# Weighing and key fills placed behind the maxima of each cycle, and VectorE's long steps of both layers moved behind its maxima

## What is computed

```
x = x + L0_xattn(ln(x), ctx); x = x + L0_attn(ln(x)); x = x + L0_ffn(ln(x))
# L1 cross attention, by far the largest part: 32 x 16 heads x 64 x 1601 scores
k, v = ctx @ Wk.T + bk, ctx @ Wv.T + bv
p = softmax(q / 4 @ k.T);  x = x + (p @ v) @ Wo.T + bo
# L1 "attn": x1 = pw(causal_conv(rmsnorm(ln(x)))) + ..., hg = normed @ w_hg,
#   h_t = a_t * h_(t-1) + v_t  (a scan over the 64 tokens), x2 = h @ w_out + x1, then silu(n @ wg) * (n @ wv) @ w_ff_out
# L1 "ffn": xq = round(x / scale); h = gelu(xq @ W1q); hq = round(h / scale(h)); out = hq @ W2q
```

## Time and profile before

| | |
|---|---|
| time, median of 3 runs (lowest, highest) | 2437.48 us (2430.88, 2440.86) |
| the profiled execution | 2435.09 us, its span 2433.2 us |
| TensorE busy | 2077.9 us, 85% |
| VectorE, ScalarE, GpSimd busy | 1412.0, 1053.6, 519.1 us |
| granted TensorE clock, mean | 0.933 of 2.4 GHz |
| first scores, last scores | 119.96 us, 2350.44 us |

### The profile page before, as it was taken

One profiled execution on the slowest core, in us unless ns is written; L12 is line 12 of the kernel. 1 busy time (PEld: TensorE's weight loads), 2 busy tenths in 40 slices (PEclk: granted clock), 3 DMA queues, 4 the chain that ended last, 5 costly groups with the idle time before them and its releaser, 6 DMA issues.

```text
span 2433.2 us, 72895 instructions
## 1 busy us (share of the span) xinstructions
PE 2077.9 (85%) x31670; PEld 1652.4 (68%) x31686; DVE 1412.0 (58%) x2625; ACT 1053.6 (43%) x2167; POOL 519.1 (21%) x836
## 2 busy tenths in 40 slices
PE   3798988898889899888988988888998889889864
PEld 2676776776767677776777767667776666667643
DVE  3556666656657664665567556565666555554533
ACT  2354445444445444445454444545434343444331
POOL 1222221212222122222212122221222211222100
PEclk7899998899999999999999999989999999999985
DMA  6334332333223243242333232233232202122121
GB/s 194 142 109 159 108 125 92 107 103 123 99 91 112 90 141 116 102 141 71 111 102 116 95 132 98 74 112 116 84 102 88 66 28 86 61 83 64 47 75 44
DMA packets 99115, 243.93 MB, mean 100 GB/s; under 512 B 13168, under 2 KB 19440, under 8 KB 98800
## 3 DMA queue, kind: packets, MB, share of 16 engines
q1 hardware_dynamic: 98800, 239.26, 29.1%
HBM read 235.94 MB, written 3.15 MB: 98 GB/s over the span
## 4 chain that ended last, share of the span: by engine, by line
PE 67%; DVE 23%; issue 5%; ACT 3%; SPq 1%; POOL 1%; DMA 0%; DVEq 0%; POOLq 0%; ACTq 0%
PE M L722 12%; DVE mx L1417 11%; PE SC L917 7%; PE O L940 7%; PE SC L894 7%; PE M L715 7%; PE X L744 4%; PE SC L910 3%; PE M L744 2%; DVE oT L1432 2%; PE X L1000 2%; PE M L785 1%; PE X L971 1%; PE M L749 1%; DVE V L1238 1%
## 5 line engine op out<-in xcount | busy, mean ns | idle before, releaser
L1110 ACT ACTIVATE probT<-SC 128x512 f32<-128x512 f32 (+1 forms) x1024 | 445.6, 522 | 323.5 <-PE SC L917 322.7
L1417 DVE TENSOR_REDUCE mx<-SC 128x4 f32<-128x1600 f32 (+1 forms) x256 | 467.2, 1825 | 167.2 <-PE SC L894 167.1
L1059 ACT ACTIVATE kT<-M,bk 128x400 f32<-128x400 f32 (+1 forms) x224 | 133.4, 595 | 639.8 <-PE M L715 639.7
L722 PE MATMUL M<-wvs,rowsT 128*128 128x256 f32 x2496 | 381.4, 304 | 0.8 <-issue 0.8
L715 PEld LDWEIGHTS M<-rowsT,wks 128*128 128x128 f32 x1536 | 265.6, 190 | 146.5 <-issue 141.5
L715 PE MATMUL M<-rowsT,wks 128*128 128x400 f32 (+1 forms) x1536 | 351.4, 364 | 11.2 <-PE SC L917 10.4
L722 PEld LDWEIGHTS M<-wvs,rowsT 128*128 128x128 f32 x2496 | 333.7, 202 | 31.9 <-issue 12.3
L1238 DVE TENSOR_TENSOR V<-M,bv 128x256 f32<-128x256 f32 (+1 forms) x448 | 160.1, 399 | 271.1 <-PE M L722 266.7
L582 POOL TENSOR_TENSOR rowsT<-raw,rowsT 128x768 fp32r<-128x768 f32 (+1 forms) x128 | 253.5, 1981 | 211.4 <-ACT rowsT L1160 210.4
L894 PE MATMUL SC<-kT,bdq 32*128 32x400 f32 (+1 forms) x2048 | 245.6, 548 | 20.8 <-ACT probT L1110 14.3
L917 PE MATMUL SC<-bdq,kT 32*128 32x128 f32 x6656 | 257.8, 290 | 0.0
(11 more groups left out here) (250 smaller groups left out, 2532.2 us busy)
## 6 DMA issues: line engine op xcount, KB each, us to landing
ring<-in_ws_dram SPq DMA_DIRECT2D x428, 256.0 KB, 4.5
raw<-in_ctx_dram SPq DMA_DIRECT2D x32, 1601.0 KB, 6.7
summed<-in_ctx_dram SPq DMA_DIRECT2D x60, 800.5 KB, 4.5
ring<-rounded_scratch SPq DMA_DIRECT2D x64, 256.0 KB, 6.2
out_dram<-x SPq DMA_DIRECT2D x16, 128.0 KB, 2.2
x<-in_x_dram SPq DMA_DIRECT2D x1, 1792.0 KB, 10.4
kT<-in_ctx_dram SPq DMA_DIRECT2D x2, 800.5 KB, 8.8
rounded_scratch<-wround SPq DMA_DIRECT2D x8, 128.0 KB, 2.0
```

Of the source, the lines that this page charges most:

```text
L722: mm = pe.matmul(bank[:, (t - 2 * a) * D:(t - 2 * a + 1) * D], rowsT[xp][:, cc, t * P:(t + 1) * P], wvs[wp][:, cc, :], start=(at == cc == ...
L1059: act.activation(keys(n, c)[:, k0:k0 + kn], bank[:, 0:kn], ACT.Identity, bias=bk[:, c:c + 1]).then_inc(m_used[f % 2], 1)
L1110: act.activation(probT[step % 2][0:w, j, 0:len(ts), :].rearrange("p t q -> p (t q)"), SC[0:w, j, 0:len(ts) * P], ACT.Exp)\
L1417: dve.tensor_reduce(mx[c][:, :, n], SC[:, :, 0:KCH[n][1]], AX.X, ALU.max).then_inc(max_used, 1)
```

## The change

1. On TensorE, `maxima` moves ahead of `weigh`. Place "B" keeps only `max0` and `max1` and is ahead of the maxima, right behind "A"; sums, output projection and `wabs` go to a place "C" behind `weigh`; the old "C" is now "D".
2. No key chunk is filled ahead of the maxima any more. The first fill of k = 7 is gone; key (1, 2) is second in k = 7, and key (1, 3) second in k = 0 of its own batch, a cycle later. ScalarE drains all keys; 32 drains leave VectorE for ScalarE.
3. On VectorE, the convolution, the recurrence, the rounding of `xq`, `hidden_scale` with the rounding of `hq`, and the start of layer 0's softmax stand behind the maxima and the second drains (`layer1_later`, `softmax_start`). Their readers on TensorE come a cycle later: the steps of layer 1 from `gow` on (q = 9 to 17 become 10 to 18), those of layer 0 from `l0_pt0` on. The `up` and `up0` fills with their Gelu move from k = 7 of an odd batch to k = 0 of the even one.
4. On GpSimd the low part stands ahead of the layers' steps, and the recurrence's operand (`gates`) at the end of the cycle.

```diff
-FIRST = [[value(5)], [value(6)], [value(0)], [value(1)], [value(2)], [value(3)], [value(4)], [key(1, 2)]]
-SECOND = [[], [key(0, 0)], [key(0, 1)], [key(0, 2)], [key(0, 3)], [key(1, 0)], [key(1, 1)], [key(1, 3)]]
+FIRST = [[value(5)], [value(6)], [value(0)], [value(1)], [value(2)], [value(3)], [value(4)], []]
+SECOND = [[key(1, 3)], [key(0, 0)], [key(0, 1)], [key(0, 2)], [key(0, 3)], [key(1, 0)], [key(1, 1)], [key(1, 2)]]
+OWN = value(5), value(6), key(1, 3)
...
-L1_X = {(5, "A"): "conv_in", (6, "A"): "pw", (7, "A"): "gru_in", (7, "C"): "hg0", (8, "A"): "hg1", (9, "A"): "gow",
-        (10, "A"): "ff_in", (10, "C"): "ff0", (11, "A"): "ff1", (11, "C"): "ff2", (12, "A"): "fow", (14, "A"): "xq",
-        (15, "A"): "up0", (17, "A"): "hq", (17, "C"): "down"}
+L1_X = {(5, "A"): "conv_in", (6, "A"): "pw", (7, "A"): "gru_in", (7, "D"): "hg0", (8, "A"): "hg1", (10, "A"): "gow",
+        (11, "A"): "ff_in", (11, "D"): "ff0", (12, "A"): "ff1", (12, "D"): "ff2", (13, "A"): "fow", (15, "A"): "xq",
+        (16, "A"): "up0", (18, "A"): "hq", (18, "D"): "down"}
...
@@ tensor
-                    for what in x_fills(b, k, "A"):
-                        fill_x(what)
+                    for place in "AB":
+                        for what in x_fills(b, k, place):
+                            fill_x(what)
+                    maxima(b, k)
                     if k:
                         weigh(b, k - 1)
                     else:
                         weigh(b - 1, STEPS - 1)
-                    for what in x_fills(b, k, "B"):
+                    for what in x_fills(b, k, "C"):
                         fill_x(what)
-                    maxima(b, k)
                     for what in pieces(b, k, "second"):
                         fill(what)
-                    for what in x_fills(b, k, "C"):
+                    for what in x_fills(b, k, "D"):
                         fill_x(what)
...
@@ vector
-                    for what in x_fills(b, k, "A"):
-                        drain_x(what)
-                    for t, q in second_layer(b, k):
-                        if q == 16:
-                            hidden_scale(t)
+                    for place in "AB":
+                        for what in x_fills(b, k, place):
+                            drain_x(what)
+                    maxima(b, k)
                     if k == 0 and 0 <= b - 1 < B:
                         dve.wait_ge(o_ready, b)
                         dve.tensor_copy(osb[:, :, :], Og).then_inc(o_used, 1)
-                    for what in x_fills(b, k, "B"):
+                    for what in x_fills(b, k, "C"):
                         drain_x(what)
-                    maxima(b, k)
                     for what in pieces(b, k, "second"):
                         drain(what)
+                    for t, q in second_layer(b, k):
+                        layer1_later(t, q)
                     for i, q in first_layer(b, k):
                         if q == 4:
+                            softmax_start(i)
+                        if q == 5:
                             softmax_end(i)
```

More of the change, by code:

```diff
@@ L179, in pieces @@
     for what in (FIRST, SECOND)[half == "second"][k]:
-        batch = b if what in (value(5), value(6)) else b + 1
+        batch = b if what in OWN else b + 1
         if 0 <= batch < B and b >= -1:
@@ L205, in x_fills @@
     if place == "B":
+        if k == 3 and 0 <= b < B:
+            yield "max1", b
+        if k == 7 and 0 <= b + 1 < B:
+            yield "max0", b + 1
+    if place == "C":
         if k == 1 and 0 <= b - 1 < B:
@@ L236, in use, with count @@
             USES.append((what, cycle, name))
+    def count(what, number, kind, cycle):
+        number[what] = len(number)
+        use(what, kind, cycle)
     for b, k in SLOTS:
         cycle = STEPS * b + k
-        for half in ("first", "second"):
-            for what in pieces(b, k, half):
-                NUMBER[what] = len(NUMBER)
-                use(what, what[1], cycle)
-            for place in ("AB" if half == "first" else "C"):
-                for what in x_fills(b, k, place):
-                    XNUMBER[what] = len(XNUMBER)
-                    use(what, what[0], cycle)
+        for what in pieces(b, k, "first"):
+            count(what, NUMBER, what[1], cycle)
+        for place in "ABC":
+            for what in x_fills(b, k, place):
+                count(what, XNUMBER, what[0], cycle)
+        for what in pieces(b, k, "second"):
+            count(what, NUMBER, what[1], cycle)
+        for what in x_fills(b, k, "D"):
+            count(what, XNUMBER, what[0], cycle)
         for kind, n in weight_passes(b, k):
```

103 lines of the change are left out of this document (50 added, 53 removed).

## The result

The changed kernel takes 2442.3 us (median of 20 runs, 2434.0 to 2453.2) against 2433.5 us before (20 runs): a ratio of 1.0033, 95% interval 1.0020 to 1.0046. That is no change by the 0.5% bound that the prediction set, and a small loss where a gain of 31 us was forecast (2437 to 2406). The profiled span is 2436.6 us.

A forecast was written before the change was run, and what follows sets the result against it. TensorE bounds the kernel, its idle time mostly scores waiting for VectorE's reduction of the maxima. From 2435.1 us, 17 for the pairs and 14 for layer 0 leave 2404, stated as 2406 for the median; range 2355 to 2460, likeliest case 2380 to 2423.

The forecast's parts named there:

- The walk of the pair: Batches 28 and 29: TensorE's idle time goes from 15.9 to 14.8 us, 1.1 us a pair, 17 us over 15 pairs.
- the term for layer 0: Eleven pairs with layer 0: first fills cover new waits, 19 us, less about 5 for a context sum; net 14 us gained.
- The bank X: In k = 7 and k = 3, `max0` or `max1` waits for the drained bank: 1.7, 0.7 and 0.75 us.
- The clock: Granted clock over the pair taken as unchanged by the change; mean between first and last scores stays within 0.94 to 0.97.
- rival B: Stalls of over 2 us in the pair each bring half clock behind them; slower, 2479 us; chance 0.22.
- C: Even exchange: a longer chain (2433 us), or gaps 1 us a pair larger and nothing from layer 0 (2435); chance 0.20.
- A, the plain reckoning: Counting only the waits, weighing and key fill cover about 120 of 156.4 us; 2346 us or less; chance 0.16.
- the second scan behind a low part: Recurrence: the second scan starts behind a low part of 1.8 us, `gow` comes 1.8 us later in 15 pairs, +27 us.
- Maxima for exponentials: TensorE's maxima waiting for ScalarE's exponentials rise from 14 to 80 to 110 us, largest in k = 1 of even batches.
- Idle time: TensorE between first and last scores: 256 us comes out between 215 and 250, otherwise the prediction is wrong.
- longest relative loser: Layer 1's half of k = 7 was to be the cycle that loses most in relation.
- The table load: k = 1, even batches: a load costs 1.28 us without a further drain, and the maxima wait about 2.45 us.

The follow-up runs named there:

- c_l1_early: The changed kernel with layer 1's steps on VectorE and GpSimd and their readers back as before, only layer 0's softmax late: 2415.1 us.
- l_hidden_early: The changed kernel with the hidden values' scale back ahead of the maxima of k = 1, their rounding at the start of k = 2: 2423.2 us.
- o_not0: The kernel before with the change's TensorE order, key table and places of X, but the weighing ahead of the maxima in k = 0: 2407.3 us.
- p_not_x: j_mix146 with the weighing behind the maxima in k = 2 and 5 as well, so ahead of them in k = 0, 3 and 7 alone: 2345.1 us.
- f_no_switch: The changed kernel with Tanh in place of Gelu in both halves of the hidden values, so the two table loads a tile go: 2408.0 us.
- j_mix146: The kernel before with the change's key table and the weighing behind the maxima only in k = 1, 4 and 6: 2349.3 us.
- k_mix1: The kernel before with the change's key table and the weighing behind the maxima in k = 1 alone: 2352.3 us.
- q_late_mix: The whole change, all late steps kept, with the weighing behind the maxima in k = 1, 4 and 6 alone: 2439.8 us.

## Why the prediction was wrong

The change is a sum of gains and losses. By the medians, in this one order of steps (another order would share them out otherwise, see the end of this section): key table -33 us; weighing behind the maxima in k = 1, 2, 4, 5 and 6, with the sums behind the reduction, -55; the same in k = 3 and 7, +62; in k = 0, +2; the softmax late, +6; layer 1's steps late, +27. Together +9.

**The walk of the pair held.** Forecast 14.8 us of idle time in batches 28 and 29, measured 13.6; cycle by cycle within 0.35 us but for k = 7, even, with 1.06 in place of 1.7. The named waits of that pair came as said: exponentials behind the table load in k = 1, `hq` 1.93 us, `xq` 1.5, bank X 0.7. The pair gained 3.6 us instead of 1.1, 2.3 of it idle time. Over cycles 216 to 247, two pairs, it was 5.4 a pair, 2.5 of it idle time.

**The step that failed is the term for layer 0**: "Net 14 us. Bounds: none of the cover (0) and all of it". It had the wrong sign, and the loss lay outside these bounds, the least of which was no gain. (The cover was written as about 60 cycles by 0.3 us, 19 us; the product is 18.) With the pair's 1.1 us, the prediction had 26 us less for the stretch with layer 0; it took 20.3 more. The step counted what layer 0's fills cover and a context sum on ScalarE. It didn't ask who waits for VectorE in the next cycle: layer 0's normalisations (a first step of a cycle, TensorE's reader right behind it) and the softmax's end stood behind layer 1's late steps. In cycles 16 to 186 the waits for n and SA went from 11.5 to 51.4 us together, and the idle time of that stretch rose by 23.6. c_l1_early and l_hidden_early show it as the cause: one step of layer 1 put back on VectorE gives 19 us, all of layer 1's put back 27. For layer 1 I had followed the readers of every late step; for layer 0, whose steps are in the same queue, only its own moved one.

**The walk as a frame hid two things.** It took the pair's idle time before and after as one sum and called it an exchange. It was one, but between parts that could be had apart. The table's 33 us were in the walk as 2.4 us a k = 0, all but given back; the runs show that most of them are clock, in one execution each. The bank X, "1.7 us in k = 7 even, 0.7 in k = 7 odd, 0.75 in k = 3", was seen and priced by its waits; its clock (22.6 of 52.6 us between the two windows of o_not0 and p_not_x) was not.

**The clock.** "I take the clock as unchanged" came true for the whole, 0.95 before and after, so rival B didn't happen. It did in parts: behind the 2.77 us wait in k = 1 the weighing and the key fill ran at 1.39 and 2.39 us. But such waits had been in the kernel before: behind one of 1.95 us the granted clock was 0.52, behind one of 2.41 us the matmuls ran at full speed.

**The rivals.** C came nearest in time (2433 to 2435; measured 2442), and that is partly luck. One of its forms had gaps 1 us a pair larger and nothing from layer 0: the gaps came out 1.2 us a pair smaller, and layer 0's stretch lost. Its other mechanism, the second scan behind a low part, did not come: all 16 second scans took 0.69 us. A, the plain reckoning, was wrong for the change. With the late steps and the X places out the time came near A's 2346 (2345), but not by A's sum: that has 89 us less waiting, and p_not_x has 37 us less idle time and 52 less busy time than before.

**The forecasts of the views.** Scores for the reduction, 9.0 us: right (under 40). Maxima for exponentials, 75.9, just below 80 to 110. `hq` 26.5, within 25 to 35 by luck: 10.4 us of it lie behind the last scores, where 9.5 had been before, and 9 tiles brought the other 16.1, up to 2.3 each. `xq` 17.7 (13.1 between the scores), below 25 to 35; `gow` 9.8 (6.7), below about 15. X bank 34.2 within 20 to 40. Idle time 271.9, outside 215 to 250: the mark that I had set for being wrong. Mean clock 0.95, inside. The longest relative loser was not layer 1's k = 7 (7.04 to 7.62 us in batch 29) but k = 2 of batch 28, with `hq` in it: 8.68 to 11.18 us.

**The table load.** The sum went by the row, 1.28 us, and had 2.46 us for the wait in k = 1; it measured 2.77. ScalarE there, in the changed kernel:

```profile
2138.61 1.28 ACT L1121 ACT_TABLE_LOAD   x1
2139.91 2.06 ACT L1121 ACTIVATE probT<-SC 128x512 f32<-128x512 f32 x4
```

The load begins 0.02 us behind the instruction before it and the exponentials 0.02 us behind the load. Without the switch the wait is 1.39 us shorter and not 2.7: one load stands in this chain, and in f_no_switch the exponentials follow the high part directly, with the scores done 0.1 us before. This case's runs agree with the row, not with the drain of 1.38 us on top that the Trainium skill states in "ScalarE: Activation LUTs", section "What ACT_TABLE_LOAD costs".

Left open: why the late steps cost 33 us where all weighing is behind the maxima, and 68 and 90 in the other orders. By stretches they cost 38, 61 and 73 us in cycles 16 to 186 and, in cycles 216 to 247, gain 6 in the first order and cost 11 and 9 in the other two. The traces suggest that they also move the Gelu out of k = 7, where it drains bank X just ahead of `max0` (the 25.9 us above have no like in the changed kernel), so that two losses partly stand in for each other; no run changed the Gelu's place alone.

## What to carry to other kernels

When a step is moved back in an engine's queue, list every instruction that then starts behind it in the next cycles, of all layers and tiles in flight, and not only the moved step's own readers; one stretch with less in it, however well it is reckoned, doesn't stand for one in which two layers share the engine. Try the parts of a compound change alone and per place in the cycle before giving up on an exchange: here two parts of it, one of them in five of eight cycles, are worth 3.6%, and the whole is worth nothing. Look at what runs behind a long wait of TensorE as well. Taking a wait of 2.5 us out of k = 1 gave as much again in busy time (27.6 us idle, 27.2 busy), taking one of 2.8 us out with the table load only a fifth of that (24.2 and 4.9): read it from the trace, it isn't a fixed share.

## What was unexpected of the hardware

The same 31,000 matmuls between first and last scores were busy for 1912 to 1989 us, by their order and the waits between them: 77 us, as much as the idle times differ (208 to 287). One doesn't follow the other: j_mix146 has 14.4 us less idle time than k_mix1 and 13.5 more busy. Part of that is the execution that was profiled: j_mix146's four had a mean granted clock of 0.951 to 0.961, the profiled one 0.951, k_mix1's 0.957 to 0.959.

A rounding with one input of 128x1024 took 2.17 us beside a GpSimd instruction of 2.35 us that began 0.73 us before it, and 0.69 alone. The scans have two inputs and do the same. That agrees with the Trainium skill, "SBUF — State Buffer", section "Who interferes with whom", which counts `tensor_scalar` in its two-port modes among those that the shared ports block. It was not what decided: in q_late_mix 2 of the 32 scans took over 1 us, in the changed kernel 10, and the two kernels take the same time.
